# Rotary keys and queries by one projection and a lane shuffle in a four-layer cross-attention kernel

## The chip, the cores and the metric

The kernel runs on one core of a Trainium2 chip. The metric is the device time of one execution in microseconds, as the median of three runs. A core has TensorE (PE; PEld is its weight load), VectorE (DVE), ScalarE (ACT), GpSimd (POOL) and SyncE (SP, which here issues DMAs). Each takes its own list of instructions in order, and they wait for one another by semaphores.

## The reference

Four layers, each with cross-attention and a feed-forward part, on x of 16 batches x 112 tokens x 256, with a context of 16 x 375 x 256. All is float32. The attention of layer l is added to x with a gate:

```python
x = x + tanh(g_xattn[l]) * attention_l(layernorm(x), ctx)   # l = 0..3
x = x + tanh(g_ffn[l])   * ffn_l(layernorm(x))
# layer 0: 8 heads of 32; then layernorm(q + out) through a KAN layer:
#   silu(y) @ base_w.T + b_splines(y) @ scaled_spline_w.T   (8 bases per input)
# layer 1: 16 heads of 64, mask over keys
# layer 2: 16 heads of 16, rotary positions on q and k:
q = q * cos + rotate_half(q) * sin      # rotate_half(x) = [-x[8:], x[:8]] in each head
k = k * cos + rotate_half(k) * sin
# layer 3: 16 heads of 16, additive mask on the scores
```

The feed-forward parts (a tree of soft decisions, a dense mixture, two routed mixtures) are not touched.

## The kernel before

`attention_stage` builds one layer's attention for all engines; the Python loops are unrolled. `batches` goes over t = -1 .. 15 and one or two more. In iteration t the attention of batch t runs, the projections of batch t + 1 are made, and the output of batch t - 1 (in layer 0 also of t - 2) is finished.

Heads are worked in groups of four: four groups in layers 2 and 3, two in layer 0. In group i TensorE's `body` issues, in this order: `scores` of the next group (four products into the four banks of `sc_ps`), `pv` of the group before, and then three turns (`turn`, L723: four transposes of probabilities each) with the projections that `CYCLES` names between them. `CYCLES[layer][i][pos]` lists the uses that stand at place pos: before the first turn (0), after turn 0 (1), after turn 1 (2), after turn 2 (3). The names: `k`, `v`, `q` are projections; `kr` and `qr` are the same projections with the rows of the weights exchanged within each head, so that their result is the rotary partner; `xT` is the transpose of the normalized x; `rt` that of the reciprocal row sums; `out` the output projection; `lnt` the transpose of layer 0's normalized residual; `kan` its KAN product (a silu part, L679, and 16 spline parts, L683). `LAG` says to which batch each belongs.

All turns and uses take their PSUM room from `full_ps`, three banks handed out in turn over the list (`ring`). `bank_free` makes TensorE wait before each use until what was last in its bank has been copied out (`copied`).

Who copies: ACT copies k, v, q, xT and rt and turn 0 of each group; DVE copies turns 1 and 2 (`copy_turn`), and in layer 2 k, kr, q and qr, each in one instruction that adds the bias and multiplies by the cosine or sine table (L994, L1001). GpSimd adds the two products to kT (`rope_add`, L528), and DVE adds those of q and writes the two halves (`halve_q`). ACT's order in a group of layers 2 and 3 is: exponentials 0 and 1, copy of turn 0, exponentials 2 and 3, then the copies of places 1 to 3. DVE's is: row maxima (L1041; with a mask L1035), in group 0 `divide_o` and `norm_stats`, the use of place 1, turn 1, in group 0 `norm_apply` (L965), the use of place 2, turn 2, the use of place 3. GpSimd's in an iteration is: `power` (L516, the inverse root for the norm), rope_add of chunk 0, `add_bias` (L522), `spread` (the reciprocals, L535), rope_add of chunk 1. Without a mask the scores of a group wait until all four exponentials have read `sc_ps`; with one they wait for DVE's masked copy.

SyncE only loads the context, two batches ahead, and weights of later stages.

The lines of the profile are those of the code below.

Of the kernel before, what the change touches and what calls it, by code (L numbers as in the profile page):

```python
# [22 lines left out]
P = 128  # L23
# [156 lines left out]
def batches(eng, body, tail):  # L180

    for b in range(-1, B + tail):
# [7 lines left out]
        [[], [], [("lnt",), ("kan",)], [("v", 1, 0), ("qtok",), ("v", 2, 0), ("rest",)]]],  # L190
# [15 lines left out]
LAG = {"k": 1, "kr": 1, "v": 1, "xT": 1, "q": 1, "qr": 1, "qtok": 1, "rt": 0, "turn": 0, "out": -1,  # L206
# [10 lines left out]
def attention_stage(core, layer, heads, hd, scale, rope=False, mask=None, kan=False, moe=None):  # L217
# [21 lines left out]
    for i in range(NG):  # L239
# [9 lines left out]
    plain = lambda u: u[0] in ("k", "kr", "v", "xT", "qtok") or (u[0] == "q" and layer == 1)  # L249
    on_bank = {r: [j for j in jobs if plain(j) and bank_of[j] == r] for r in range(BANKS)}  # L250
    kv = [j for j in jobs if j[0] in ("k", "kr", "v")]
# [3 lines left out]
        (u[0] in ("k", "q") and not rope)  # L255
# [5 lines left out]
    with ExitStack() as ctx:  # L261
# [8 lines left out]
        if rope:  # L270
            wqr, wkr = room([P, DC, DQ]), room([P, DC, DQ])
            weights += [(wqr, "wqrT"), (wkr, "wkrT")]
# [4 lines left out]
        if rope:  # L277
            bqr, bkr = room([P, QC]), room([P, QC])
            cos, sin = room([P, SK]), room([P, SK])
            small += [(bqr, "bqr"), (bkr, "bkr"), (cos, "cos"), (sin, "sin")]  # L280
# [56 lines left out]
        if rope:  # L337
            rot_a, rot_b = sb("rot_a", [P, 2, SK]), sb("rot_b", [P, 2, SK])
            qrot_a, qrot_b = sb("qrot_a", [P, DC, S]), sb("qrot_b", [P, DC, S])
# [51 lines left out]
        if rope:  # L391
            s_ropek = sig("rope_k_ready", QC)
            s_rope_q = sig("rope_q_parts", 2 * DC)
            s_qsum = sig("q_summed", 1)
# [14 lines left out]

        def job(j, b):  # L410

            return s_job.sem, s_job.at(b, index_of[j])

        def copied(u, b):
# [5 lines left out]
            if kind == "q" and rope:  # L420
                return s_rope_q.sem, s_rope_q.at(b, DC - 1)
            if kind == "qr":
                return s_rope_q.sem, s_rope_q.at(b, 2 * DC - 1)
# [56 lines left out]
        with nc.Block() as block:  # L480
# [30 lines left out]
            def _(pool):  # L511
# [12 lines left out]
                def rope_add(b, par, c):  # L524

                    for kind in ("k", "kr"):
                        pool.wait_ge(*copied((kind, c), b))
                    pool.tensor_tensor(kT[:, par, c, :], rot_a[:, c, :], rot_b[:, c, :], ALU.add)\  # L528
                        .then_inc(s_ropek.sem, 1)

# [43 lines left out]
                def body(t, par):  # L574
# [18 lines left out]
            def _(pe):  # L593
# [13 lines left out]
                def run_use(u, t, par):  # L607
# [4 lines left out]
                    if kind in ("k", "kr"):  # L612
                        if u == kv[0]:
                            in_ctx(pe, b, par)
                        w = wk if kind == "k" else wkr
                        for c in range(DC):
                            mm = pe.matmul(use_ps[:, 0:SK], w[:, c, u[1] * P:(u[1] + 1) * P],  # L617
# [17 lines left out]
                    elif kind in ("q", "qr"):  # L635
                        if kind == "q":
                            pe.wait_ge(*copied(("xT",), b))
                        w = wq if kind == "q" else wqr
                        for i in range(qn):
                            f = u[1] + i  # L640
                            for c in range(DC):
                                mm = pe.matmul(use_ps[:, i * S:(i + 1) * S], w[:, c, f * P:(f + 1) * P],
# [28 lines left out]
                    else:  # L671
                        kan_output(b, use_ps[0:S, 0:D])

                def kan_output(b, kan_ps):
# [3 lines left out]
                    for c in range(DC):  # L678
                        pe.matmul(kan_ps, silu[:, c, :], base_w[:, c, :], start=(c == 0), stop=False)  # L679
                    for c in range(DC):  # L680
# [6 lines left out]
                def scores(b, par, i):  # L687
                    chunk = q_of(par, head(i, 0))[3]
                    if rope:
                        pe.wait_ge(s_ropek.sem, s_ropek.at(b, chunk))  # L690
# [55 lines left out]
                def body(t, par):  # L746
                    for i in range(NG):
# [1631 lines left out]
```

## Time and profile before

| | |
|---|---|
| median of 3 runs | 3092.79 us (3087.96 to 3093.75) |
| the profiled execution | 3098.28 us, span 3096.4 us |
| PE busy in the span | 2832.2 us (91%) |
| DVE, ACT, POOL busy | 1588.6 us, 1277.7 us, 520.8 us |
| attention of layer 0 | from about 14 to 435 us: PE 368.48 of 421 us |
| attention of layer 2 | from about 1444 to 1842 us: PE 382.03 of 398 us, POOL 56.01, clock 0.99 |
| attention of layer 3 | from about 2324 to 2690 us: PE 336.94 of 366 us, clock 0.96 |

The busy time of an engine is the sum of its instructions. The clock is TensorE's granted clock as a share of full speed. The last three lines come from the view that gives busy times in chosen stretches of the span.

### The profile page before, as it was taken

What the parts mean: (1) busy time and instruction counts of PE and PEld (TensorE: products, weight loads), DVE (VectorE), ACT (ScalarE), POOL (GpSimd) and SP (SyncE); (2) the same over time, 40 slices, a digit from 0 to 9 for tenths busy, and PEclk for the clock granted to TensorE, in tenths of its full rate; (3) what the DMA queues carried; (4) which work ended last, traced back from release to release, by engine and by line L of the source; (5) the groups of instructions that cost most, each with busy time, mean ns of one, the idle gap of its engine ahead of it and who ended that gap; (6) DMA issues with size and microseconds to landing.
All of it is one profiled execution on the core that took longest, in us unless ns stands there. A gap on an engine that the chain in (4) does not pass through costs nothing. (4 is left out here: it accounts for less than half of the span.)

```text
span 3096.4 us, 58811 instructions
## 1 busy us (share of the span) xinstructions
PE 2832.2 (91%) x20592; PEld 2152.5 (70%) x20592; DVE 1588.6 (51%) x4239; ACT 1277.7 (41%) x3555; POOL 520.8 (17%) x441
## 2 busy tenths in 40 slices
PE   6999968999999999698999975999988999859998
PEld 4777645666666666556766655999985667648887
DVE  4767634555555555345777763233326777532222
ACT  4676621444344334212555541333336666412221
POOL 1555530000000000000111110222210000002222
PEclk8999989999999999589999995999999999769999
DMA  3000010000000000010000003999971000048887
GB/s 111 16 16 21 6 66 2 12 12 7 12 12 12 7 12 1 28 38 7 16 16 20 18 7 106 348 328 327 329 246 33 22 22 17 23 142 279 280 285 222
DMA packets 92887, 269.66 MB, mean 87 GB/s; under 512 B 25977, under 2 KB 51722, under 8 KB 78314
## 3 DMA queue, kind: packets, MB, share of 16 engines
q1 hardware_dynamic: 75434, 244.63, 23.1%
q0 software_dynamic: 13632, 18.62, 3.0%
q10 hardware_dynamic: 3616, 3.67, 0.4%
q8 instruction: 130, 2.13, 0.3%
q14 instruction: 75, 0.61, 0.1%
HBM read 250.23 MB, written 18.48 MB: 87 GB/s over the span
## 5 line engine op out<-in xcount | busy, mean ns | idle before, releaser
L723 PEld LDWEIGHTS a_full_ps<-ident,a_probs 112*125 112x125 f32 x2688 | 369.7, 190 | 153.2 <-issue 59.6
L2146 PE MATMUL e_ab_ps<-e_xT,e_w 128*128 128x128 f32 (+1 forms) x3968 | 467.3, 278 | 5.4 <-DMA e_w<-in_L3f_w 2.3
L2146 PEld LDWEIGHTS e_ab_ps<-e_xT,e_w 128*128 128x128 f32 (+1 forms) x3968 | 453.6, 189 | 24.4 <-issue 11.9
L723 PE MATMUL a_full_ps<-ident,a_probs 112*125 112x112 f32 x2688 | 422.2, 282 | 30.1 <-ACT a_kT L788 9.5
L1061 DVE COPY a_pT<-a_full_ps 125x448 f32<-125x448 f32 x448 | 277.4, 621 | 281.0 <-PE a_full_ps L723 279.7
L821 ACT ACTIVATE a_probs<-a_masked,a_negmax 112x375 f32<-112x375 f32 x512 | 305.4, 598 | 278.0 <-DVE a_negmax L1035 278.0
L617 PE MATMUL a_full_ps<-attention_room 128*128 128x375 f32 x1024 | 371.0, 490 | 1.1 <-DVE a_v L1006 0.6
L625 PE MATMUL a_full_ps<-attention_room 128*125 128x256 f32 (+1 forms) x960 | 331.1, 474 | 8.5 <-ACT a_qT L813 3.1
L821 ACT ACTIVATE a_probs<-a_sc_ps,a_negmax 112x375 f32<-112x375 f32 x384 | 217.9, 579 | 125.7 <-DVE a_negmax L1041 125.6
L1035 DVE CUSTOM_DVE_ANT_0 a_masked<-a_sc_ps,a_mask_add 112x375 f32<-112x375 f32 x512 | 249.8, 544 | 36.8 <-PE a_sc_ps L710 36.4
L741 PEld LDWEIGHTS a_o_ps<-a_pT,a_v 125*32 125x32 f32 (+1 forms) x5376 | 164.7, 118 | 125.4 <-issue 124.3
L710 PE MATMUL a_sc_ps<-a_kT,a_qT 32*112 32x375 f32 (+1 forms) x1792 | 241.5, 513 | 3.3 <-ACT a_probs L821 3.2
L617 PEld LDWEIGHTS a_full_ps<-attention_room 128*128 128x128 f32 x1024 | 182.9, 194 | 80.7 <-issue 5.7
L2157 PE MATMUL e_y_ps<-e_w,e_hid 128*128 128x256 f32 x992 | 233.0, 383 | 0.0
L625 PEld LDWEIGHTS a_full_ps<-attention_room 128*125 128x125 f32 x960 | 167.2, 189 | 90.5 <-issue 66.2
L516 POOL TENSOR_TENSOR a_rstd<-a_rstd,minus_half 112x1 f32<-112x1 f32 x64 | 35.1, 549 | 1113.8 <-DVE a_rstd L958 1106.7
L741 PE MATMUL a_o_ps<-a_pT,a_v 125*32 125x112 f32 (+1 forms) x5376 | 216.6, 266 | 5.8 <-DVE a_pT L1061 3.8
L2190 ACT ACTIVATE e_silu<-e_ab_ps,e_b 128x128 f32<-128x128 f32 x280 | 102.4, 367 | 242.7 <-PE e_ab_ps L2146 227.8
L2157 PEld LDWEIGHTS e_y_ps<-e_w,e_hid 128*128 128x128 f32 x992 | 179.9, 190 | 32.2 <-issue 12.1
L1041 DVE TENSOR_REDUCE a_negmax<-a_sc_ps 112x2 f32<-112x750 f32 x192 | 171.3, 934 | 58.8 <-PE a_sc_ps L710 58.8
L2080 POOL DMA_INDIRECT p_sums<-e_y_out,p_put x71 | 112.6, 1586 | 512.1 <-DVE e_y_out L2230 288.7
L2217 DVE SCALAR_TENSOR_TENSOR e_hid<-e_ab_ps,e_b,e_silu 128x128 f32<-128x128 f32 x280 | 97.9, 351 | 172.1 <-ACT e_silu L2190 172.1
(247 smaller groups left out, 3654.2 us busy)
## 6 DMA issues: line engine op xcount, KB each, us to landing
e_w<-in_L2f_w SPq DMA_DIRECT2D x105, 1024.0 KB, 6.9
e_w<-in_L3f_w SPq DMA_DIRECT2D x72, 704.0 KB, 5.3
e_w<-in_L3f_w SPq DMA_DIRECT2D x36, 768.0 KB, 5.8
attention_room<-in_ctxT SPq DMA_DIRECT2D x64, 375.0 KB, 3.0
e_b<-in_L2f_b SPq DMA_DIRECT2D x35, 128.0 KB, 8.4
p_rows<-r_kept SPq DMA_DIRECT2D x32, 112.0 KB, 1.9
p_sums<-x_all ACTq DMA_DIRECT2D x2, 1792.0 KB, 18.1
attention_room<-in_L0x_spline_wT SPq DMA_DIRECT2D x1, 2048.0 KB, 9.9
```

Of the source, the lines that this page charges most:

```text
L617: mm = pe.matmul(use_ps[:, 0:SK], w[:, c, u[1] * P:(u[1] + 1) * P], ctxT[:, par, c, :], start=(c == 0), stop=(c == DC - 1))
L625: mm = pe.matmul(use_ps[0:KT, 0:v_width], ctxT[:, par, c, k * KT:(k + 1) * KT], wv[:, c, part * v_width:(part + 1) * v_width], start=(c == ...
L710: pe.matmul(sc_ps[:, a, 0:SK], lhs, kT[r:r + k, par, c, :], start=True, stop=True)\
L723: mm = pe.transpose(full_ps[0:KT, bank_of["turn", i, k], (j % 4) * S:(j % 4 + 1) * S], probs[:, i % 2, a, t * KT:(t + 1) * KT], ident[0:S, ...
L741: mm = pe.matmul(o_ps[a % WIDE * VW:(a % WIDE + 1) * VW, block * S:(block + 1) * S], v[:, par, t, head(i, a), :], pT[:, i % 2, KC * a + t, :],
L821: act.activation(probs[:, i % 2, a, 0:SK], src, ACT.Exp, bias=negmax[:, m:m + 1], scale=-1.0 if mask else 1.0, accum_out=rowsum[:, par, n: ...
L1035: dve.tensor_tensor_reduce(out=masked[:, i % 2, a, :], in0=sc_ps[:, a, 0:SK], in1=bias, scale=-1.0, scalar=FLT_MAX, op0=ALU.add, op1=ALU.m ...
L1041: dve.tensor_reduce(negmax[:, m:m + 2], sc_ps[:, 2 * a:2 * a + 2, 0:SK], AX.X, ALU.max, negate=True).then_inc(s_max.sem, 1)
L1061: dve.tensor_copy(pT[:, i % 2, 4 * k:4 * (k + 1), :], full_ps[0:KT, bank_of["turn", i, k], 0:4 * S] .rearrange("p (j s) -> p j s", j=4)).t ...
L2080: pool.indirect_dma_start(plan.sums, bass.IndirectOffsetOnAxis(plan.put[:, t:t + 1], 0), y_out[:, t % 2, :], None, compute_op=ALU.add).the ...
L2146: mm = pe.matmul(ab_ps[0:rows[f], (par * FC + f) % RING, i * SLOTS:(i + 1) * SLOTS], w[:, par, c, f * P:f * P + rows[f]], xT[:, c, :], sta ...
L2157: mm = pe.matmul(y_ps[:, par, 0:D], hid[0:rows[f], f, :], w2[0:rows[f], par, f, :], start=(f == 0), stop=(f == FC - 1))
```

## The change

In layer 2, `kr` and `qr` and their weights go away. ACT copies k and q with their bias from PSUM to SBUF (`k_raw`, `q_raw`). DVE makes the partners from these copies by `stream_shuffle`, which exchanges partitions within each 32 (`PARTNERS`; `partners_k`, `partners_q`), after turn 1 of the group in which k or q stands. GpSimd multiplies by the cosines and by the sines and adds, for k (`rope_add`) and now for q too (`rope_q`, between add_bias and spread). The list of layer 2 becomes nearly that of layer 3.

In layers 2 and 3 (`divided`), ACT copies the use of place 1 between exponentials 1 and 2 instead of after exponential 3. In layer 0, the silu part of `kan` stands ahead of `lnt`, and the spline parts follow lnt; with that kan and lnt exchange their banks.

```diff
-        [[], [], [("lnt",), ("kan",)], [("v", 1, 0), ("qtok",), ("v", 2, 0), ("rest",)]]],
+        [[], [], [("kan",), ("lnt",)], [("v", 1, 0), ("qtok",), ("v", 2, 0), ("rest",)]]],
...
-    2: [[[], [("k", 0)], [("kr", 0)], [("xT",)]],
-        [[], [("q", 0)], [("out",)], [("qr", 0)]],
-        [[], [("v", 0, 0)], [("v", 1, 0)], [("v", 2, 0)]],
-        [[], [("k", 1)], [("kr", 1)], [("rt",)]]],
+    2: [[[], [("k", 0)], [("v", 0, 0)], [("xT",)]],
+        [[], [("q", 0)], [("out",)], []],
+        [[], [("v", 1, 0)], [], []],
+        [[], [("k", 1)], [("v", 2, 0)], [("rt",)]]],
...
+PARTNERS = [p // 16 * 16 + (p + 8) % 16 for p in range(32)]
...
                 def rope_add(b, par, c):
-                    for kind in ("k", "kr"):
-                        pool.wait_ge(*copied((kind, c), b))
+                    step = lambda k: (s_ropek.sem, s_ropek.at(b, c * ROPE_STEPS + k))
+                    pool.wait_ge(*copied(("k", c), b))
+                    pool.sem_inc(s_tick[3].sem, 1)
+                    pool.tensor_tensor(rot_a[:, c, :], k_raw[:, c, :], cos[:], ALU.mult).then_inc(s_ropek.sem, 1)
+                    pool.wait_ge(s_kpart.sem, s_kpart.at(b, c))
+                    pool.sem_inc(s_tick[3].sem, 1)
+                    pool.tensor_tensor(rot_b[:, c, :], k_partner[:, c, :], sin[:], ALU.mult).then_inc(s_ropek.sem, 1)
+                    pool.wait_ge(*step(ROPE_SIN))
+                    pool.sem_inc(s_tick[3].sem, 1)
                     pool.tensor_tensor(kT[:, par, c, :], rot_a[:, c, :], rot_b[:, c, :], ALU.add)\
                         .then_inc(s_ropek.sem, 1)
+                def rope_q(b):
+                    table = lambda t: t[:, 0:S].unsqueeze(1).to_broadcast([P, DC, S])
+                    pool.wait_ge(s_qf.sem, s_qf.at(b, QC - 1))
...
+                    pool.tensor_tensor(qrot_a[:], q_raw[:], table(cos), ALU.mult).then_inc(s_ropeq.sem, 1)
+                    pool.wait_ge(s_qpart.sem, s_qpart.at(b))
...
+                    pool.tensor_tensor(qrot_b[:], q_partner[:], table(sin), ALU.mult).then_inc(s_ropeq.sem, 1)
...
+                    pool.tensor_tensor(qfull[:], qrot_a[:], qrot_b[:], ALU.add).then_inc(s_ropeq.sem, 1)
...
                         add_bias(t + 1)
+                    if rope and exists(t + 1):
+                        rope_q(t + 1)
...
                     else:
-                        kan_output(b, use_ps[0:S, 0:D])
+                        kan_silu(b, use_ps[0:S, 0:D])
...
                             for u in uses_at(t, i, pos):
                                 run_use(u, t, par)
+                            if ("kan",) in cycles[i][pos] and exists(t - 2):
+                                kan_splines(t - 2)
...
                     if kind == "k":
                         f = u[1]
-                        act.activation(kT[:, par, f, :], use_ps[:, 0:SK], ACT.Identity,
+                        if rope and has(b, 1):
+                            act.wait_ge(*rotated(b - 1, f))
+                            act.sem_inc(s_tick[0].sem, 1)
+                        act.activation(k_raw[:, f, :] if rope else kT[:, par, f, :], use_ps[:, 0:SK], ACT.Identity,
...
+                        if divided:
+                            copies(t, par, i, 1)
                         for group in groups:
                             exps(*group, (2, 3))
...
-                        for pos in range(1, TURNS + 1):
+                        for pos in range(2 if divided else 1, TURNS + 1):
                             copies(t, par, i, pos)
...
+                def partners_k(b, c):
+                    if has(b, 1):
+                        dve.wait_ge(*rotated(b - 1, c))
+                        dve.sem_inc(s_tick[1].sem, 1)
+                    dve.wait_ge(*copied(("k", c), b))
+                    dve.sem_inc(s_tick[1].sem, 1)
+                    dve.stream_shuffle(k_partner[:, c, :], k_raw[:, c, :], PARTNERS).then_inc(s_kpart.sem, 1)
...
                 def halve_q(b, par):
                     if rope:
-                        dve.wait_ge(s_rope_q.sem, s_rope_q.at(b, 2 * DC - 1))
...
-                        dve.tensor_tensor(qfull[:], qrot_a[:], qrot_b[:], ALU.add).then_inc(s_qsum.sem, 1)
-                        dve.wait_ge(s_qsum.sem, s_qsum.at(b))
+                        dve.wait_ge(s_ropeq.sem, s_ropeq.at(b, ROPE_SUM))
...
                         if exists(t):
                             copy_turn(t, i, 1)
+                        if rope and exists(t + 1):
+                            if ("k", 0) in cycles[i][1]:
+                                partners_k(t + 1, 0)
+                            if ("k", 1) in cycles[i][1]:
+                                partners_k(t + 1, 1)
+                            if ("q", 0) in cycles[i][1]:
+                                partners_q(t + 1)
                         if i == 0 and exists(t + 1):
                             norm_apply(t + 1)
```

`rotated(b, c)` is the semaphore value at which GpSimd's sum for chunk c of k is done. `partners_q` is made like `partners_k`, in one shuffle of 224 columns.

## Rows read from the trace of the kernel before

**Rows 1.** Timeline, layer 2, one batch: start us, us, engine, line, operation, [idle before].
```profile
1604.94 0.90 PE L710 MATMUL a_sc_ps<-a_kT,a_qT 32*112 32x375 f32 x8
...
1607.01 1.44 PE L617 MATMUL a_full_ps<-attention_room 128*128 128x375 f32 x4
...
1608.29 0.59 PE L723 MATMUL a_full_ps<-ident,a_probs 112*125 112x112 f32 x4
1608.71 1.44 PE L617 MATMUL a_full_ps<-attention_room 128*128 128x375 f32 x4
...
1610.41 0.35 PE L632 MATMUL a_full_ps<-ident,a_xn 112*128 112x112 f32 x2
...
1610.70 0.90 PE L710 MATMUL a_sc_ps<-a_kT,a_qT 32*112 32x375 f32 x8
...
1616.70 0.90 PE L710 MATMUL a_sc_ps<-a_kT,a_qT 32*112 32x375 f32 x8
...
1623.28 0.90 PE L710 MATMUL a_sc_ps<-a_kT,a_qT 32*112 32x375 f32 x8
...
1629.04 0.90 PE L710 MATMUL a_sc_ps<-a_kT,a_qT 32*112 32x375 f32 x8
```

**Rows 2.** Timeline, layer 2, last batch, without projections.
```profile
1821.84 0.90 PE L710 MATMUL a_sc_ps<-a_kT,a_qT 32*112 32x375 f32 x8
...
1825.31 0.58 ACT L821 ACTIVATE a_probs<-a_sc_ps,a_negmax 112x375 f32<-112x375 f32 x1
...
1826.68 0.90 PE L710 MATMUL a_sc_ps<-a_kT,a_qT 32*112 32x375 f32 x8 [1.74 <-ACT a_probs L821]
```

**Rows 3.** Timeline, layer 2, group 0 of the batch of rows 1, DVE and GpSimd.
```profile
1608.91 0.55 POOL L516 TENSOR_TENSOR a_rstd<-a_rstd,minus_half 112x1 f32<-112x1 f32 x1 [2.73 <-DVE a_rstd L958]
...
1609.28 0.61 DVE L1061 COPY a_pT<-a_full_ps 125x448 f32<-125x448 f32 x1
1609.81 0.41 DVE L965 TENSOR_SCALAR a_xn<-x_all,a_mv,a_rstd 112x256 f32<-112x256 f32 x1
...
1610.95 0.98 POOL L528 TENSOR_TENSOR a_kT<-a_rot_a,a_rot_b 128x375 f32<-128x375 f32 x1 [1.49 <-DVE a_rot_b L994]
```

**Rows 4.** Timelines of DVE and GpSimd, layer 0, at two places.
```profile
70.50 1.11 DVE L1134 SCALAR_TENSOR_TENSOR a_near<-a_sq,a_near 128x896 f32<-128x896 f32 x1
...
70.62 2.53 POOL L544 TENSOR_TENSOR a_sq<-a_near 128x896 f32<-128x896 f32 x1
...
207.75 1.67 POOL L544 TENSOR_TENSOR a_sq<-a_near 128x896 f32<-128x896 f32 x1
...
208.26 1.31 DVE L965 TENSOR_SCALAR a_xn<-x_all,a_mv,a_rstd 112x256 f32<-112x256 f32 x1
```

**Rows 5.** Timeline, layer 3, end of one group 0.
```profile
2492.36 1.04 PE L625 MATMUL a_full_ps<-attention_room 128*125 128x256 f32 x4
...
2493.05 0.56 ACT L788 ACTIVATE a_kT<-a_full_ps,attention_room 128x375 f32<-128x375 f32 x1
2493.44 0.41 DVE L965 TENSOR_SCALAR a_xn<-x_all,a_mv,a_rstd 112x256 f32<-112x256 f32 x1
...
2493.76 0.66 PE L723 MATMUL a_full_ps<-ident,a_probs 112*125 112x112 f32 x4 [0.35 <-ACT a_kT L788]
...
2494.25 0.35 PE L632 MATMUL a_full_ps<-ident,a_xn 112*128 112x112 f32 x2
```

**Rows 6.** Timeline, layer 0, lnt and the uses around it.
```profile
221.87 0.38 PE L669 MATMUL a_full_ps<-ident,a_resn 112*128 112x112 f32 x2 [0.78 <-DVE a_resn L1103]
...
222.09 1.03 PE L679 MATMUL a_full_ps<-attention_room,a_silu 128*112 128x256 f32 x4
...
222.96 7.10 PE L683 MATMUL a_full_ps<-attention_room,a_bases 128*112 128x256 f32 x32
...
230.10 0.48 DVE L1077 SCALAR_TENSOR_TENSOR x_all<-a_full_ps,gates,x_all 112x256 f32<-112x256 f32 x1 [4.06 <-PE a_full_ps L683]
...
230.32 1.04 PE L625 MATMUL a_full_ps<-attention_room 128*125 128x256 f32 x4
...
231.19 1.03 PE L647 MATMUL a_full_ps<-attention_room,a_xT 128*112 128x256 f32 x4
```

More of the change, by code:

```diff
@@ L204 @@
 BANKS, TURNS = 3, 3
-LAG = {"k": 1, "kr": 1, "v": 1, "xT": 1, "q": 1, "qr": 1, "qtok": 1, "rt": 0, "turn": 0, "out": -1,
+ROPE_COS, ROPE_SIN, ROPE_SUM, ROPE_STEPS = 0, 1, 2, 3
+PARTNERS = [p // 16 * 16 + (p + 8) % 16 for p in range(32)]
+LAG = {"k": 1, "v": 1, "xT": 1, "q": 1, "qtok": 1, "rt": 0, "turn": 0, "out": -1,
        "oback": -1, "lnt": -1, "kan": -2}
@@ L248, in attention_stage @@
     index_of = {j: i for i, j in enumerate(jobs)}
-    plain = lambda u: u[0] in ("k", "kr", "v", "xT", "qtok") or (u[0] == "q" and layer == 1)
+    plain = lambda u: u[0] in ("k", "v", "xT", "qtok") or (u[0] == "q" and layer == 1)
     on_bank = {r: [j for j in jobs if plain(j) and bank_of[j] == r] for r in range(BANKS)}
-    kv = [j for j in jobs if j[0] in ("k", "kr", "v")]
+    kv = [j for j in jobs if j[0] in ("k", "v")]
     v_width = min(DQ, 512)
@@ L254, in attention_stage @@
     on_scalar = lambda u: u[0] in ("xT", "rt") or (u[0] == "v" and layer != 1) or \
-        (u[0] in ("k", "q") and not rope)
+        u[0] in ("k", "q")
     OC = heads * hd // P
@@ L277, in attention_stage @@
         if rope:
-            bqr, bkr = room([P, QC]), room([P, QC])
             cos, sin = room([P, SK]), room([P, SK])
-            small += [(bqr, "bqr"), (bkr, "bkr"), (cos, "cos"), (sin, "sin")]
+            small += [(cos, "cos"), (sin, "sin")]
         if hd == 16:
@@ L634, in run_use @@
                         mm.then_inc(s_job.sem, 1)
[L635 to L638, printed above, removed]
+                    elif kind == "q":
+                        pe.wait_ge(*copied(("xT",), b))
                         for i in range(qn):
@@ L679, in kan_output, with kan_splines @@
                         pe.matmul(kan_ps, silu[:, c, :], base_w[:, c, :], start=(c == 0), stop=False)
+                def kan_splines(b):
+                    kan_ps = full_ps[0:S, bank_of[("kan",)], 0:D]
                     for c in range(DC):
@@ L689, in scores @@
                     if rope:
-                        pe.wait_ge(s_ropek.sem, s_ropek.at(b, chunk))
+                        pe.wait_ge(*rotated(b, chunk))
                     elif layer != 1:
@@ L796, in copy_use @@
                         if has(b, 1):
-                            act.wait_ge(*job([j for j in jobs if j[0] in ("q", "qr", "qtok")][-1], b - 1))
+                            act.wait_ge(*job([j for j in jobs if j[0] in ("q", "qtok")][-1], b - 1))
                         act.activation(xT[:, :, :], use_ps[:, 0:DC * S].rearrange("p (c s) -> p c s", c=DC),
@@ L988, in copy_use @@
                     dve.wait_ge(*job(u, b))
-                    if kind in ("k", "kr"):
-                        f = u[1]
-                        if has(b, 1):
-                            dve.wait_ge(s_ropek.sem, s_ropek.at(b - 1, f))
-                        dst, bias, table = (rot_a, bk, cos) if kind == "k" else (rot_b, bkr, sin)
-                        dve.scalar_tensor_tensor(out=dst[:, f, :], in0=use_ps[:, 0:SK], scalar=bias[:, f:f + 1],
-                                                 in1=table[:], op0=ALU.add, op1=ALU.mult).then_inc(free, 1)
-                    elif kind in ("q", "qr"):
-                        if has(b, 1):
-                            dve.wait_ge(s_qsum.sem, s_qsum.at(b - 1))
-                        dst, bias, table = (qrot_a, bq, cos) if kind == "q" else (qrot_b, bqr, sin)
-                        for c in range(DC):
-                            dve.scalar_tensor_tensor(out=dst[:, c, :], in0=use_ps[:, c * S:(c + 1) * S],
-                                                     scalar=bias[:, c:c + 1], in1=table[:, 0:S], op0=ALU.add,
-                                                     op1=ALU.mult).then_inc(s_rope_q.sem, 1)
-                    elif kind == "v":
+                    if kind == "v":
                         _, k, part = u
```

55 lines of the change are left out of this document (31 added, 24 removed).

## The prediction

> **What bounds the kernel now.** I read the busy table of the page first: TensorE is busy for nine tenths of the span, so the question is always which wait of TensorE goes. Then I read the timeline of one batch in each of the three attention layers that the change touches, because a share over the span says nothing about one loop. Times below are counted from the start of the scores (L710) that open a group; each group ends where the next scores start.
>
> Layer 2 [rows 1]: a batch is four groups of 5.76, 6.00, 6.58 and 5.76 us, 24.10 us in all (1604.94 to 1629.04), and TensorE runs its list nearly without a gap. From scores to the first projection 2.07 us, k 1.28, a turn 0.42, then kr and another turn, the transpose of xn (xT) 0.29. In the middle of the layer ACT and DVE have slack.
>
> A second limit is visible only where the projections run out [rows 2]: there scores follow scores after 4.84 us, with TensorE waiting 1.74 us for the exponentials. sc_ps is one buffer: scores, row maxima, exponentials 0 and 1, the copy of a turn, exponentials 2 and 3 (the third starts at 3.47), next scores. Nothing shortens this loop, and whatever ACT does inside it lengthens it.
>
> Layer 3 [rows 5] has the same list without kr and qr. In groups 0 and 3 turn 2 needs the bank that k used, and ACT copies k only after exponential 3. The v product starts at 2492.36 and, being 0.87 long [rows 6], ends at 2493.23; the turn starts at 2493.76. That is 0.53 us lost; group 3, with rt in place of xT, has the same, and I take 0.5 there.
>
> Layer 0 [rows 6]: the transpose lnt waits for the residual (0.78 us of it as a gap before L669) while the silu product, whose input is there, stands behind it.
>
> **Layer 2, part by part.** Removed from TensorE per batch: two kr products of 1.28 us and qr (taken as 1.0), about 3.5 us. Removed from DVE: four multiply-adds of 375 columns, four of 112 and the q sum. Added on ACT: k copied twice, 0.56 us each [rows 5], and q in two pieces, which I take as 0.6 together. On DVE: three shuffles. On GpSimd: two more operations of 375 columns for each k chunk (0.98 each [rows 3]) and three of 224 for q, about 0.6 each by columns. GpSimd then works some 9 us of a batch, and its k and q are due 2 to 10 us after they are ready. They are hidden, unless they hinder DVE. The new waits of ACT and DVE for the sums of the batch before are met a batch's length earlier.
>
> The shuffle is in no row. Below, I bound it by a 256-column DVE instruction, 0.41, above by the 448-column copy, 0.61 [rows 3]; for 375 columns I take 0.5. The Trainium skill (VectorE: DVE Perf Modes, "The perf-mode tier table") gives a shuffle about 2400 ns for 2048 elements; an estimate from it is 0.44 us for 375, and the sum would be 1 us shorter by it.
>
> Now the groups, with the new list of projections:
>
> Group 3 (k, v, rt). TensorE needs 5.76 less kr 1.28 plus v 0.87, or 5.35. The exponential loop takes k's copy in: k ends at 3.51, its copy at about 4.12, exponential 2 moves from 3.47 to about 4.05, and 4.84 becomes about 5.4. I take 5.4.
>
> Group 1 (q, out). TensorE would need 6.00 less 1.0, but the loop has 4.84 plus two q copies less a small overlap, about 5.35. The loop decides.
>
> Group 2 (v). The loop with one v copy of 0.37 is 5.2, and TensorE needs less than 4.4. The loop decides.
>
> Group 0 (k, v, xT) is where a new wait comes. xT needs norm_apply on DVE. Before, norm_apply runs from 4.87 to 5.28 and TensorE wants it at 5.47 [rows 1, 3], so nobody waits. Now TensorE wants xT at 5.06, and the shuffle of k stands in front of norm_apply: copy_turn starts at about 4.0, ends and lets the shuffle in at 4.55, norm_apply could start at 5.05. But GpSimd has ended its power at 4.52 [rows 3] and is multiplying k by the cosines until about 5.5, and the two engines exclude each other for such operations: in layer 0 the same L965 that takes 0.41 us alone takes 1.31 beside L544 and ends 0.15 after it [rows 3, 4]. So norm_apply ends at 5.65 to 6.0, I take 5.7; xT follows 0.15 later and the scores 0.29 after that: 6.15. Does the sine multiplication slip in first? Rows 4 have such a meeting: L1134 on DVE asks at 70.50 while L549 ends, ends itself at 71.61, and the L544 that GpSimd had queued takes 2.53 us instead of 1.67. DVE got in between, so I let DVE in after the cosines. Its delay of group 0 also delays copy_turn(0,2), which group 1 needs only 0.83 after its start, so nothing more.
>
> Sum: 6.15 + 5.35 + 5.2 + 5.4 = 22.1 against 24.1, 2.0 us a batch, and 15 full batches: 30 us. The bounds for group 0 are 5.75 (no meeting, shuffle 0.41) and 7.1 (DVE also waits for the sines), which gives 36 and 16 us. The start of the stage I take as even: two half-clock products less, against ACT and three GpSimd operations in place of one ahead of the first scores. The end, where no batch follows, does not change. The halving of q waits on GpSimd now; q is copied at 4.1 of group 1, three times 0.6 later it is summed, and the halving comes at about 2.7 of group 2. What stands behind that wait (two copies of turns and so the next pv) is safe by about 2 us.
>
> **Layer 3.** k's copy moves ahead of exponentials 2 and 3. TensorE's turn 2 then follows v at once: 0.5 us saved in group 3. In group 0 the next limit is xT again: norm_apply ends at 2493.85, xT starts at 2494.25 and could start at about 2494.0, so I count 0.25, not 0.53 [rows 5]. The later exponentials do no harm, because scores here wait for DVE's masked copies and turn 1 of the next group comes several us later. 0.75 a batch, 15 batches: 11 us. Bounds: 0.3 (a second wait behind the bank) and 1.0, so 4 to 15.
>
> **Layer 0.** The silu product (222.09 to 222.96, 0.87) moves into the wait: lnt stays where it is, the splines start 0.87 earlier. The banks of kan and lnt are exchanged by this. v(1) now needs the bank of kan, which is free when DVE has updated x_all, at 230.10 + 0.48 = 230.58, and TensorE wants it at 230.32 [rows 6]; 0.26, and 0.1 more for wait and weight load that were hidden, come back. Before, that update had the whole v product (0.87, to 231.19) as cover. Net 0.5 us in 13 batches and 0.87 in the last two: 8 us. Bounds 0 and 12.
>
> **Total.** The profiled execution took 3098.28 us (span 3096.4), 5.5 above the median of 3092.79. Its stages lose 30 + 11 + 8 = 49 us: 3049 for such an execution, and taken off the median 3044.
>
> **Rivals.**
> 1. GpSimd keeps the port through cosines and sines (its instructions follow each other within 0.05 us). Group 0 becomes 7.1 and layer 2 saves 16 us: 3092.8 - 16 - 19 = 3058. Against it stands the meeting at 70.5.
> 2. The shuffles are held off by GpSimd too. Then the shuffle of group 0 ends at about 5.9, norm_apply at 6.2, the group at 6.65; group 3 gets 0.15 longer. Layer 2 saves 1.35 a batch, 20 us: 3054. No row shows a DVE instruction of that kind beside GpSimd. The Trainium skill (SBUF, State Buffer, "Who interferes with whom") says that a DVE instruction with one SBUF input outside the two-port modes does not contend, and its tier table gives the shuffle only the 1x mode; by it this rival falls and the sum stays at 22.1.
> 3. Everything is cover: norm_apply gets through ahead of the cosines, layer 3 gets its full 1.0, layer 0 its 0.87. 36 + 15 + 12 = 63: 3030, the lower side.
> 4. The orders give less than they say: the waits of layers 0 and 3 are replaced by others of the same length (0 and 4 us left). 30 + 4: 3059.
> 5. Slower: the shuffle is dear. Be D its time for 375 columns. Above 0.6 it adds D - 0.75 in group 0, above 1.0 D - 1.0 in group 3 (copy_turn(3,2) then misses the next pv), and in group 1 about 0.6 D - 0.8: 2.55 less than 2.6 D in all. The forecast gain of 3.3 a batch is gone at D = 2.25; slower by over 0.2% needs 2.4, or 6.4 ns a column, where DVE's rows have 1.4 to 1.6 with the fixed part. At D = 3 the time would be 3044 + 15 x 5.25 = 3123.
>
> **Chances.** Forecast 0.45, rivals 0.14, 0.11, 0.12, 0.12 and 0.05 in order; 0.01 for the unforeseen. The range runs from 3028 to 3064: it holds the forecast with its bounds and rivals 1 to 4 mostly. A measurement of this kernel tells about 0.2% (6 us) from no change. Faster 0.92, same 0.03, slower 0.05.
>
> **What will show it.** Distances between the scores in layer 2: about 6.15, 5.35, 5.2, 5.4. In groups 1 and 2 the scores should be released by the exponentials (a gap before L710 put down to ACT), which the steady part has nowhere now. Before xT a wait for DVE's xn, and L965 at 0.6 us or more in layer 2. In layer 3 the wait for ACT's k gone, and the batch 0.75 us shorter. In layer 0 the batch 0.5 us shorter, and v(1) waiting for x_all. I am wrong if group 0 stays below 5.8 or above 6.6, if groups 1 and 2 fall below 5, or if any layer's batch is longer than before.

## The result and the profile after

| | before | after |
|---|---|---|
| median | 3090.86 us (3087.96 to 3093.75, 4 runs) | 3044.99 us (3041.45 to 3048.90, 4 runs) |
| profiled execution (span) | 3098.28 us (3096.4) | 3048.90 us (3047.1) |
| PE, DVE busy | 2832.2, 1588.6 us | 2778.5, 1549.9 us |
| ACT, POOL busy | 1277.7, 520.8 us | 1301.9, 608.1 us |

The ratio is 0.9852, with a 95% interval of 0.9835 to 0.9869: 46 us faster. The forecast was 3044, taken as 49 us off the median of 3092.79; the fourth run of the kernel before has moved that median to 3090.86.

I read the after trace as I read the other: by the distance from one scores to the next. Steady values in us, good to 0.01 or 0.02, with the span from the stage's first scores to its last:

| | before | forecast | after | span before, after |
|---|---|---|---|---|
| layer 2, groups 0 to 3 | 5.76, 6.00, 6.58, 5.76 | 6.15, 5.35, 5.2, 5.4 | 5.92, 5.33, 5.09, 5.48 | 375.17, 342.70 |
| layer 2, a batch | 24.10 | 22.1 | 21.82 | |
| layer 3, groups 0 to 3 | 5.95, 4.94, 4.11, 5.95 | 5.7, 4.94, 4.11, 5.45 | 5.72, 4.94, 4.11, 5.40 | 325.62, 314.13 |
| layer 0, a batch | 22.79 | 22.3 | 22.33 | 348.94, 336.55 |

One batch of layer 2 in the timeline, the counterpart of [rows 1] and [rows 3]: start us, us, engine, line, operation, [idle before]. Scores are now L735, turns L748, xT L656, norm_apply L1001.

```profile
1606.55 0.85 POOL L530 TENSOR_TENSOR a_rot_a<-a_k_raw,attention_room 128x375 f32<-128x375 f32 x1
1606.61 0.59 DVE L1038 STREAM_SHUFFLE a_k_partner<-a_k_raw 128x375 f32<-128x375 f32 x1
1607.09 0.46 DVE L1001 TENSOR_SCALAR a_xn<-x_all,a_mv,a_rstd 112x256 f32<-112x256 f32 x1
1607.38 0.88 POOL L533 TENSOR_TENSOR a_rot_b<-a_k_partner,attention_room 128x375 f32<-128x375 f32 x1
1607.70 0.39 PE L656 MATMUL a_full_ps<-ident,a_xn 112*128 112x112 f32 x2 [0.37 <-DVE a_xn L1001]
1608.01 0.90 PE L735 MATMUL a_sc_ps<-a_kT,a_qT 32*112 32x375 f32 x8
...
1612.50 0.60 ACT L855 ACTIVATE a_probs<-a_sc_ps,a_negmax 112x375 f32<-112x375 f32 x1
...
1613.34 0.90 PE L735 MATMUL a_sc_ps<-a_kT,a_qT 32*112 32x375 f32 x8
...
1618.42 0.90 PE L735 MATMUL a_sc_ps<-a_kT,a_qT 32*112 32x375 f32 x8 [0.72 <-ACT a_probs L855]
...
1622.54 0.57 ACT L855 ACTIVATE a_probs<-a_sc_ps,a_negmax 112x375 f32<-112x375 f32 x1
...
1623.09 0.58 ACT L855 ACTIVATE a_probs<-a_sc_ps,a_negmax 112x375 f32<-112x375 f32 x1
...
1623.90 0.90 PE L735 MATMUL a_sc_ps<-a_kT,a_qT 32*112 32x375 f32 x8
```

Group 0 started at 1602.09, so norm_apply is asked for at 5.00, ends at 5.46 and xT starts at 5.61, after a wait of 0.37 that before did not have. In groups 1, 2 and 3 the scores follow the end of the fourth exponential by 0.23 or 0.24 (1612.50 + 0.60 against 1613.34; 1623.09 + 0.58 against 1623.90), as where the projections run out in [rows 2]. The exponential loop has become the bound. Only group 2 shows it as a gap of TensorE. In group 3 the margin is small: TensorE's own list would let the scores start about 0.1 us earlier (turn 2 starts at 1623.07; with 0.42 for it and 0.29 for rt the scores could follow at 1623.78). In group 3 k's copy (0.57, at 1622.07) moved the third exponential to 4.12 after the scores; without a copy it is at 3.47.

The view of waits, TensorE, 1500 to 1750 us (waited for: us in total, times, longest), has these two on top:

```profile
PE a_sc_ps L735 <- ACT a_probs L855: 8.7, 12, 0.7
PE a_full_ps L656 <- DVE a_xn L1001: 4.0, 11, 0.4
```

Both waits were forecast. One sign did not come: norm_apply should have taken 0.6 us or more in layer 2, and takes 0.46.

Groups of instructions of the same stretch (xcount | busy us, mean ns | idle before) give the prices that no row of before had:

```profile
L536 POOL TENSOR_TENSOR a_kT<-a_rot_a,a_rot_b 128x375 f32<-128x375 f32 x23 | 22.6, 981 | 4.1 <-POOL a_rot_b L533 4.1
L530 POOL TENSOR_TENSOR a_rot_a<-a_k_raw,attention_room 128x375 f32<-128x375 f32 x22 | 20.3, 924 | 10.6 <-ACT a_k_raw L818 10.6
L1038 DVE STREAM_SHUFFLE a_k_partner<-a_k_raw 128x375 f32<-128x375 f32 x22 | 12.9, 586 | 0.0
L1047 DVE STREAM_SHUFFLE a_q_partner<-a_q_raw 128x224 f32<-128x224 f32 x12 | 4.9, 412 | 0.5 <-issue 0.4
```

Layer 3, end of one group 0, the counterpart of [rows 5]. The turn (2490.01) follows v (2489.13 + 0.88) at once, and what is late next is xT, by 0.17:

```profile
2489.13 1.04 PE L649 MATMUL a_full_ps<-attention_room 128*125 128x256 f32 x4
...
2490.01 0.59 PE L748 MATMUL a_full_ps<-ident,a_probs 112*125 112x112 f32 x4
2490.21 0.41 DVE L1001 TENSOR_SCALAR a_xn<-x_all,a_mv,a_rstd 112x256 f32<-112x256 f32 x1
...
2490.77 0.38 PE L656 MATMUL a_full_ps<-ident,a_xn 112*128 112x112 f32 x2 [0.17 <-DVE a_xn L1001]
```

Layer 0, the counterpart of [rows 6]. The silu product fills the wait, and v(1) now waits for the update of x_all:

```profile
214.22 1.03 PE L701 MATMUL a_full_ps<-attention_room,a_silu 128*112 128x256 f32 x4
215.16 0.38 PE L691 MATMUL a_full_ps<-ident,a_resn 112*128 112x112 f32 x2
215.37 7.10 PE L708 MATMUL a_full_ps<-attention_room,a_bases 128*112 128x256 f32 x32
...
223.05 1.13 PE L649 MATMUL a_full_ps<-attention_room 128*125 128x256 f32 x4 [0.15 <-DVE x_all L1113]
```

**Something is given back.** The spans add up to 32.5 + 11.5 + 12.4 = 56 us, the two executions differ by 49. The start of layer 0 varies from one execution to the next: its first scores came 2.45 later in this one (23.32 against 20.87; over all kernels they lie between 20.6 and 23.4), and the kernel with ACT's new order alone, whose layer 0 is that of the kernel before, has a span of 345.77 there, not 348.94. From the ninth scores to the last the layer takes 265.39 us before and 259.85 after, and each other kernel with the same order in layer 0 is within 0.06 of one or the other; so some 5.5 of the 12.4 us are the steady gain, and a part of the rest is such variation. What is really given back stands at the end of layer 2: from its last scores to the first product of the routing after it, 20.99 us (1831.76 to 1852.75) became 25.77 (1786.42 to 1812.19):

```profile
1786.42 0.90 PE L735 MATMUL a_sc_ps<-a_kT,a_qT 32*112 32x375 f32 x8
...
1788.01 1.13 PE L748 MATMUL a_full_ps<-ident,a_probs 112*125 112x112 f32 x8
1790.15 0.66 PE L748 MATMUL a_full_ps<-ident,a_probs 112*125 112x112 f32 x4 [1.01 <-ACT a_pT L861]
1791.62 1.35 PE L766 MATMUL a_o_ps<-a_pT,a_v 125*32 125x112 f32 x24 [0.81 <-DVE a_pT L1097]
1792.89 2.86 PE L748 MATMUL a_full_ps<-ident,a_probs 112*125 112x112 f32 x12
```

With the new list, turn 2 of group 2 has the bank of turn 0 and waits for ACT's copy of it (1.01; in the steady part 0.17). Before, the twelve transposes ran together. Then TensorE goes at half clock: pv, the product of probabilities and v, takes 1.35 instead of 0.78. The view of stretches (length, PE busy, ..., then the granted clock) has 0.50 for 1792 to 1800, the 1.2 GHz level, after a stretch in which TensorE was busy for 4.18 of 6 us:

```profile
1786.00:1792.00 6.00, 4.18 (x59) 3.04 (x60) 4.24 (x7) 2.76 (x9) 0.20 (x1) 0.93 0.00 0
1792.00:1800.00 8.00, 7.11 (x65) 5.49 (x55) 1.98 (x4) 0.90 (x2) 0.20 (x1) 0.50 0.01 2
```

The kernel with `rest` first (below), whose last scores start at 1786.57, runs the same work after them and stays at full clock. But it had been at the lower level just before, which the changed kernel had not (1.00 for 1776 to 1786):

```profile
1776.00:1786.00 10.00, 8.10 (x88) 5.54 (x88) 6.16 (x10) 5.72 (x19) 1.58 (x2) 0.83 0.01 2
1786.00:1792.00 6.00, 4.18 (x60) 3.01 (x63) 4.24 (x7) 2.91 (x11) 0.05 (x1) 1.00 0.00 0
```

Over all profiled executions: the eight with the new list all have the wait of 1.01 there; behind it six go at half clock to the end of the layer, one (copies last) for a part of it, and two (`rest` first, all together) stay at full clock. The three with the old list do not wait there, and both later pv take 0.78.

### The profile page after: what moved, and what is told of

Same layout as the page of the kernel before. It is cut to its first block and busy times, and to the rows that moved or that the text cites. A ratio compares the mean times of both kernels' runs of the same rounds, so it can differ in the third digit from the quotient of the medians.

```text
span 3047.1 us, 58569 instructions
## 1 busy us (share of the span) xinstructions
PE 2778.5 (91%) x20336; PEld 2123.1 (70%) x20336; DVE 1549.9 (51%) x4191; ACT 1301.9 (43%) x3619; POOL 608.1 (20%) x553
## 5 line engine op out<-in xcount | busy, mean ns | idle before, releaser
L748 PEld LDWEIGHTS a_full_ps<-ident,a_probs 112*125 112x125 f32 x2688 | 372.4, 190 | 123.6 <-issue 64.3
L748 PE MATMUL a_full_ps<-ident,a_probs 112*125 112x112 f32 x2688 | 420.0, 281 | 19.4 <-ACT a_pT L861 8.4
L641 PE MATMUL a_full_ps<-attention_room 128*128 128x375 f32 x896 | 324.8, 491 | 0.7 <-DVE a_v L1027 0.6
L735 PE MATMUL a_sc_ps<-a_kT,a_qT 32*112 32x375 f32 (+1 forms) x1792 | 241.2, 512 | 20.9 <-ACT a_probs L855 13.7
L641 PEld LDWEIGHTS a_full_ps<-attention_room 128*128 128x128 f32 x896 | 160.6, 195 | 70.9 <-issue 4.5
```

Source lines behind the costliest of these rows:

```text
L641: mm = pe.matmul(use_ps[:, 0:SK], wk[:, c, u[1] * P:(u[1] + 1) * P], ctxT[:, par, c, :], start=(c == 0), stop=(c == DC - 1))
L735: pe.matmul(sc_ps[:, a, 0:SK], lhs, kT[r:r + k, par, c, :], start=True, stop=True)\
L748: mm = pe.transpose(full_ps[0:KT, bank_of["turn", i, k], (j % 4) * S:(j % 4 + 1) * S], probs[:, i % 2, a, t * KT:(t + 1) * KT], ident[0:S, ...
```

## The experiments

Ratios are against the kernel before, run beside them: its median was 3091.96 for the two parts alone and for the norm and the cosines moved singly, 3091.11 for both moved, the two shuffles, v(1) and `rest`, 3090.86 for the new list with the copies last and for all of it together. A median or an interval tells 46 us easily, but not 2 or 3; where runs of a kernel overlap those of the changed kernel (3041.45 to 3048.90), I say so, and the distances between scores decide. My theory: TensorE's list was the bound in layer 2, the exponential loop over sc_ps (4.84 us plus ACT's copies) bounds groups 1 to 3 after the change, norm_apply bounds group 0, and the three parts of the change add up. The rivals of the forecast stand in the expectations.

**One part at a time: layer 0's order.** The kernel before with the exchange of kan and lnt and the split of `kan_output`, as in the diff of the change.

> The kernel before with layer 0's change alone (silu product ahead of lnt, splines after it). My theory: the silu product fills the wait for the residual, and v(1) then waits for the update of x_all; the period of layer 0 goes from 22.80 to 22.34 us as in the changed kernel, and the time falls by 7 to 8 us (0.25%). Rival (the gain of the changed kernel in layer 0 comes with its other edits): 22.80 stays, no difference.

Measured: 3084.48 us against 3091.96, ratio 0.9973 [0.9963, 0.9983]. Layer 0's batch is 22.34 (before 22.79), layers 2 and 3 are as before. Layer 0 is worth 7.5 us by itself, and the rival fell.

**One part at a time: ACT's order.** The kernel before with

```diff
+                        if divided:
+                            copies(t, par, i, 1)
                         for group in groups:
                             exps(*group, (2, 3))
-                        for pos in range(1, TURNS + 1):
+                        for pos in range(2 if divided else 1, TURNS + 1):
```

> The kernel before with ACT's new order alone in layers 2 and 3 (the use of place 1 copied between exponentials 1 and 2). My theory: layer 3's batch goes from 20.95 to 20.2 us, as in the changed kernel (11 us); in layer 2, still with kr and qr, only group 2 gains, because its third turn waits for ACT's copy of v(0): 6.58 to about 6.2, so 24.1 to 23.7 (6 us). Together about 17 us. Rival (the order matters in layer 2 only with the new list, and in layer 3 the wait moves elsewhere): under 5 us.

Measured: 3075.35, ratio 0.9952 [0.9936, 0.9969], 16.6 us for the expected 17. Layer 3's batch 20.18 (span 314.46): its whole gain. Layer 2's groups 5.76, 6.01, 6.00, 5.76: group 2 loses 0.58, since v(0) is copied early (1610.32) and turn 2, which before waited 0.34 for the two v copies, no longer waits. Its rows:

```profile
1610.32 0.39 ACT L794 ACTIVATE a_v<-a_full_ps 125x256 f32<-125x256 f32 x1
...
1611.46 0.59 PE L723 MATMUL a_full_ps<-ident,a_probs 112*125 112x112 f32 x4
```

**The new list without ACT's new order.** The changed kernel with these lines taken out again:

```diff
-                        if divided:
-                            copies(t, par, i, 1)
...
-                        for pos in range(2 if divided else 1, TURNS + 1):
+                        for pos in range(1, TURNS + 1):
```

> The changed kernel without ACT's new order: in layers 2 and 3 the use of place 1 is copied after exponential 3 again. My theory: layer 3 returns to 20.95 (11.5 us). In layer 2 the new list needs the early copy more than the old one: k is copied at 4.6 of group 0 instead of 3.6, the shuffle and norm_apply follow it, groups become about 6.5, 5.7, 4.84 and 5.95, 23.0 in place of 21.82 (18 us). Together about 29 us above the changed kernel, 3074. Rival (the two edits add up): layer 2 loses no more than the 0.58 a batch that the order gained in the old kernel: 9 us, and 20 us together.

Measured: 3083.77, ratio 0.9970 [0.9958, 0.9982], 38.8 us above the changed kernel. Layer 3 is back at 20.94. Layer 2's groups are 6.80, 5.91, 4.84, 6.05, 23.60 in all: the new list by itself takes only 0.5 us off a batch, the order by itself (above) 0.57, both together 2.28. The rows of group 0 (from 1618.32) show why:

```profile
1622.88 0.59 ACT L818 ACTIVATE a_k_raw<-a_full_ps,attention_room 128x375 f32<-128x375 f32 x1
1623.62 0.66 PE L748 MATMUL a_full_ps<-ident,a_probs 112*125 112x112 f32 x4 [0.49 <-ACT a_k_raw L818]
1623.65 0.59 DVE L1036 STREAM_SHUFFLE a_k_partner<-a_k_raw 128x375 f32<-128x375 f32 x1
1624.13 0.52 DVE L999 TENSOR_SCALAR a_xn<-x_all,a_mv,a_rstd 112x256 f32<-112x256 f32 x1
1624.80 0.38 PE L656 MATMUL a_full_ps<-ident,a_xn 112*128 112x112 f32 x2 [0.52 <-DVE a_xn L999]
```

k is copied after four exponentials, turn 2 waits for its bank, the shuffle waits for the copy, and norm_apply stands behind the shuffle. The two parts are one edit in layer 2. The rival (at most 20 us) fell, and my 29 us missed too: group sizes too short by 0.6 a batch, 38.8 us measured. In time the list alone is worth nothing that can be told: this kernel also holds layer 0's new order, and gains 7.1 us where that order alone gains 7.5. Layer 2's span is 4.9 us shorter (370.28 for 375.17), and 3.0 us are lost at its end (24.01 for 20.99). So the three parts of the change do not add up as I said: about 7.5 for layer 0, 16.6 for ACT's order, 0 for the list, and some 22 of the 46 us only for list and order together.

**Group 0: who makes norm_apply late?** Two things could: DVE's shuffle ahead of it, and GpSimd's cosines beside it. I took away the one, the other, and both. First norm_apply ahead of the shuffle:

```diff
+                        if i == 0 and exists(t + 1):
+                            norm_apply(t + 1)
...
                         if rope and exists(t + 1):
                             if ("k", 0) in cycles[i][1]:
                                 partners_k(t + 1, 0)
...
-                        if i == 0 and exists(t + 1):
-                            norm_apply(t + 1)
```

> The changed kernel with norm_apply ahead of the shuffle of k(0) on DVE in layer 2. Group 0 is 5.92 us in the changed kernel. Theory A (the place of the shuffle is what makes xT late): norm_apply starts 0.5 us earlier, group 0 becomes about 5.45, 7 us less in all. Theory B (port: GpSimd's multiplication by cosines starts 0.05 us before norm_apply can, and holds it off until it ends): norm_apply asks at 4.57, ends again 0.15 after the cosines, at 5.46; group 0 stays at 5.92 and the time at that of the changed kernel. I expect B for this edit alone, since both causes hold and either one suffices.

Then `rope_add` of chunk 0 behind `add_bias` on GpSimd:

```diff
-                    if rope and exists(t + 1):
-                        rope_add(t + 1, 1 - par, 0)
...
                         add_bias(t + 1)
                     if rope and exists(t + 1):
+                        rope_add(t + 1, 1 - par, 0)
```

> The changed kernel with GpSimd's three operations for k(0) behind add_bias, so that GpSimd is idle when norm_apply runs. If the port alone makes xT late (theory B alone): group 0 falls from 5.92 to about 5.45, 7 us. If the shuffle alone does (theory A), or both do: norm_apply takes 0.41 instead of 0.46 us and group 0 falls by 0.05 at most, under 1 us in all. I expect the latter.

And both:

> The changed kernel with both: norm_apply ahead of the shuffle, and GpSimd's work on k(0) behind add_bias. My theory (two causes side by side, each enough): group 0, which stayed at 5.92 with the first and fell to 5.85 with the second, now falls to where the exponential loop with k's copy holds it, 5.48 as in group 3. 0.44 a batch, 15 batches: 6.5 us below the changed kernel, about 3038. Rival (a third cause, such as power's result or the wait before the transpose): stays above 5.75.

| | norm_apply started, ended | xT started | group 0 | batch | time | ratio |
|---|---|---|---|---|---|---|
| changed kernel | 5.00, 5.46 | 5.61 | 5.92 | 21.82 | 3044.99 | 0.9852 |
| norm first | 4.53, 5.46 | 5.60 | 5.91 | 21.83 | 3044.35 | 0.9852 [0.9835, 0.9869] |
| cosines later | 5.00, 5.39 | 5.53 | 5.85 | 21.75 | 3042.66 | 0.9841 [0.9825, 0.9857] |
| both | 4.53, 4.94 | 5.09 | 5.48 | 21.34 | 3037.30 | 0.9823 [0.9807, 0.984] |

Starts and ends count from the start of the scores of group 0; norm_apply starts, in the record, when it has its input and its turn, and lasts longer than 0.41 where it is held. "Norm first" and "cosines later" share one comparison (before 3091.96), "both" has another (before 3091.11). With the norm first, DVE is held by the cosines, and ends 0.15 after them:

```profile
1607.24 0.85 POOL L530 TENSOR_TENSOR a_rot_a<-a_k_raw,attention_room 128x375 f32<-128x375 f32 x1
1607.31 0.93 DVE L1001 TENSOR_SCALAR a_xn<-x_all,a_mv,a_rstd 112x256 f32<-112x256 f32 x1
```

With both, nothing stands before it:

```profile
1607.21 0.41 DVE L1001 TENSOR_SCALAR a_xn<-x_all,a_mv,a_rstd 112x256 f32<-112x256 f32 x1
...
1607.35 0.57 ACT L855 ACTIVATE a_probs<-a_sc_ps,a_negmax 112x375 f32<-112x375 f32 x1
1607.54 0.57 DVE L1038 STREAM_SHUFFLE a_k_partner<-a_k_raw 128x375 f32<-128x375 f32 x1
1607.77 0.38 PE L656 MATMUL a_full_ps<-ident,a_xn 112*128 112x112 f32 x2
...
1608.16 0.90 PE L735 MATMUL a_sc_ps<-a_kT,a_qT 32*112 32x375 f32 x8
```

Either cause alone holds the group at 5.85 or 5.91; only without both does it fall, to 5.48. The times agree: "norm first" lies among the runs of the changed kernel, "cosines later" (3040.56 to 3045.00) overlaps them, "both" (3035.41 to 3040.94) lies below all of them. There the exponential loop takes over: 1607.35 + 0.57 + 0.24 is 1608.16. An experiment that removes one of two causes, each enough by itself, shows nothing of the other.

**What a shuffle costs there.** An extra shuffle ahead of the real one, into a spare tile:

```diff
+                    dve.stream_shuffle(k_spare[:, c, :], k_raw[:, c, :], PARTNERS)
                     dve.stream_shuffle(k_partner[:, c, :], k_raw[:, c, :], PARTNERS).then_inc(s_kpart.sem, 1)
```

> The changed kernel with every shuffle of k done twice (the first into a spare tile). This prices the shuffle where it stands, for the slower rival of the prediction. By its formula one more shuffle (0.48 us from start to start) adds about its length to group 0, since it passes the cosines: 5.92 to 6.37; group 3 is untouched up to 1.0 us of shuffles, or grows by 0.05. 7 us more in all. Rival (the shuffle is hidden behind the cosines): group 0 grows by less than 0.1. Second rival (it holds up pv in group 3): group 3 grows by 0.4 too, 14 us.

Measured: 3051.50, ratio 0.9867 [0.985, 0.9883], 6.5 us above the changed kernel for the expected 7; its four runs spread from 3047 to 3058. Group 0 is 6.33, up by 0.41; groups 1 to 3 stay. The two start 0.49 apart, the first wholly beside the cosines and no longer for it; the norm, started 0.47 after the second and past the cosines, takes 0.40:

```profile
1614.12 0.85 POOL L531 TENSOR_TENSOR a_rot_a<-a_k_raw,attention_room 128x375 f32<-128x375 f32 x1
1614.18 0.58 DVE L1039 STREAM_SHUFFLE a_k_spare<-a_k_raw 128x375 f32<-128x375 f32 x1
...
1614.67 0.58 DVE L1040 STREAM_SHUFFLE a_k_partner<-a_k_raw 128x375 f32<-128x375 f32 x1
...
1615.14 0.40 DVE L1002 TENSOR_SCALAR a_xn<-x_all,a_mv,a_rstd 112x256 f32<-112x256 f32 x1
```

The extra shuffle adds 0.49, and 0.07 of it is the hold by the cosines that the norm no longer meets.

**Is group 2 bound by the exponential loop?** v(1) copied after the exponentials again, in layer 2 only:

```diff
-                        if divided:
+                        early = divided and not (rope and cycles[i][1][0][0] == "v")
+                        if early:
                             copies(t, par, i, 1)
```

> The changed kernel with ACT's copy of v(1), the use of place 1 in group 2 of layer 2, back behind exponential 3. My theory (the loop over sc_ps bounds groups 1 and 2, TensorE's list does not): group 2 falls from 5.09 to 4.84, the length that the loop has without any copy; 3.7 us less. Rival (TensorE's list or the bank of the third turn bounds group 2): 5.09 stays.

Measured: 3041.67, ratio 0.9842 [0.9825, 0.9858], with runs that overlap those of the changed kernel. Group 2 is 4.81, the others stay. TensorE still waits for the exponentials:

```profile
1616.63 0.59 ACT L855 ACTIVATE a_probs<-a_sc_ps,a_negmax 112x375 f32<-112x375 f32 x1
...
1617.46 0.90 PE L735 MATMUL a_sc_ps<-a_kT,a_qT 32*112 32x375 f32 x8 [0.45 <-ACT a_probs L855]
```

So the loop bounds the group, and its bare length is the 4.84 of [rows 2]. For group 1, with the two q copies in the loop, no run takes the copies out; there it rests on the rows. The early copy, needed for k, costs here 0.28.

**Layer 0's residue.** `rest` in front of v(1), so that the update has a turn as cover:

```diff
-        [[], [], [("kan",), ("lnt",)], [("v", 1, 0), ("qtok",), ("v", 2, 0), ("rest",)]]],
+        [[], [], [("kan",), ("lnt",)], [("rest",), ("v", 1, 0), ("qtok",), ("v", 2, 0)]]],
```

> The changed kernel with layer 0's empty place put ahead of v(1) instead of behind v(2), so that v(1) takes the bank of lnt, qtok that of turn 2 and v(2) that of kan. My theory (v(1) waits for the update of x_all): the wait goes, the second group of layer 0 falls from 14.13 to about 13.75, the period from 22.33 to about 21.95, 5 us less in all. Rival (qtok now waits for DVE's copy of turn 2 by as much): 22.33 stays or grows.

Measured: 3042.23, ratio 0.9843 [0.9827, 0.986]. The batch is 22.03, 0.30 less, a little short of expected; the time is 2.8 us less where I expected 5, with runs that overlap those of the changed kernel. The wait of v(1) is gone:

```profile
201.22 0.49 DVE L1113 SCALAR_TENSOR_TENSOR x_all<-a_full_ps,gates,x_all 112x256 f32<-112x256 f32 x1 [3.19 <-PE a_full_ps L708]
201.44 1.04 PE L649 MATMUL a_full_ps<-attention_room 128*125 128x256 f32 x4
```

**All of it together**: norm first, cosines later, v(1) after the exponentials, `rest` first.

> All improvements that the experiments point to on top of the changed kernel: norm_apply ahead of the shuffle, GpSimd's k(0) behind add_bias, v(1) of layer 2 copied after the exponentials, the empty place of layer 0 first. By my theory they touch different groups and add up: layer 2 at 5.48 + 5.33 + 4.84 + 5.48 = 21.13 (10 us), layer 0 at 21.95 (5 us): 3030, 0.980 of the kernel before. Rival (what is freed in one group is waited for in the next): 3038 or more.

Measured: 3024.98 us (3022.9 to 3034.2, 5 runs), ratio 0.9796 [0.9779, 0.9813] to the kernel before, 20 us below the changed kernel. Layer 2's groups are 5.48, 5.31, 4.81, 5.48 (21.08, span 331.47), layer 0's batch 22.02. By batches that is 15 x 0.74 + 13 x 0.3 = 15; its profiled execution also passed the end of layer 2 at full clock, in 22.50 us (1771.68 to 1794.18) in place of 25.77. The five runs fall into two groups: three took 3022.9 to 3025.0 at a mean granted clock of 0.942 or 0.943, two took 3033.5 and 3034.2 at 0.937. The median stands in the first, so the 20 us hold more than the batches give.

## Why the prediction was right

**Which wait goes, which comes (right).** TensorE's list was the bound in layer 2, the loop over sc_ps is it now in groups 1 to 3 (tested in group 2, where v copied late gives 4.81; read from the rows in groups 1 and 3), and norm_apply in group 0. Sizes: group 1 5.33 for 5.35, group 2 5.09 for 5.2, group 3 5.48 for 5.4. In group 2 the v copy displaces the third exponential by 0.26 start to start, not by its own 0.37; in group 3 the third exponential starts at 4.12, not 4.05.

**Group 0 (right mechanism, term too large).** Forecast 6.15, measured 5.92. norm_apply was asked for at 5.00 (said 5.05), the cosines held it and it ended 0.15 after them (1606.55 + 0.85 = 1607.40, and 1607.55), as the meeting in [rows 4] had it. The mis-sized term is the cosines: 0.98 from GpSimd's sum, measured 0.85 here (1.00 in group 3; mean 0.924). That is 0.13 of the 0.23; another 0.06 is their start (4.46 for 4.52), and 0.05 that I took 5.7 where the working gave 5.65. The hold by the cosines was thereby given 0.24 (5.7 against 5.05 + 0.41), and is worth 0.07: without it the group is 5.85. The shuffle alone already makes the group late, and so do the cosines alone (5.91); the prediction did not see that taking away one would bring next to nothing.

**Rival 1 (fell).** GpSimd had the sines queued behind the cosines (its record of them starts at 1607.38), yet norm_apply ended at 1607.55: DVE got in between. The sines took 0.88 for the usual 0.85 or so.

**Rival 2 (fell).** The shuffle takes 0.58 and 0.59 with the cosines beside it (1614.18, 1606.61) and 0.57 with GpSimd idle (in the kernel with the cosines later). The Trainium skill (SBUF, State Buffer, "Who interferes with whom") says that a DVE instruction with one SBUF input outside the two-port modes does not contend with GpSimd. The trace agrees, to within those 0.02 us.

**The shuffle's price.** Taken 0.5, measured 0.586 of duration and 0.48 from its start to the next instruction's, which is what stands in the sum. The estimate of 0.44 from the Trainium skill's figure (VectorE: DVE Perf Modes, "The perf-mode tier table") is below both. Two widths, 0.586 for 375 columns and 0.412 for 224, make 1.15 ns a column and 0.15 us fixed. Rival 5 needed 2.25 us and fell.

**Rival 3 (fell).** Group 0 was held until both causes were away (5.48), layer 3 gave 0.77 a batch and not 1.0, and in layer 0 v(1) waited until `rest` stood first.

**Rival 4 (fell).** ACT's order alone gave 16.6 us (by the spans of its one profiled execution 11.2 in layer 3 and 7.8 in layer 2) and layer 0's order 7.5, where the rival left 4 and 0.

**Layer 3 (right).** 0.25 in group 0 and 0.5 in group 3 were said; 0.23 and 0.55 came, 11.5 us for 11.

**Layer 0 (right).** 0.5 in a batch said, 0.45 came; 8 us said, 7.5 measured alone.

**Layer 2's sum (too small by a tenth).** 2.28 a batch for 2.0, 32.5 us of span for 30. The start of the stage, taken as even, is not: the first distance is 4.84 for 4.41, and the first batch gains only 0.7.

**The end of layer 2 (wrong).** "The end, where no batch follows, does not change" failed. In the two profiled executions with the new list that stayed at full clock there it is 1.5 us longer (20.99 to 22.50): 1.14 by the bank wait (the second pv starts 5.20 after the last scores, for 4.06), and 0.37 because GpSimd starts the first inverse root of the routing 1.48 after its input is there, for 1.11, for which no run gives a reason. The half clock adds up to 3.3 more. In the profiled execution that is 4.8 us, against 2.5 by which layer 2's sum was too small. What the two profiled executions gained, part by part: 9.9 us up to layer 0's last scores (12.4 of span less the later start), 2.9 from there to layer 2's first, 32.5 in layer 2, -4.8 at its end, -2.3 from there to layer 3's first scores, 11.5 in layer 3, -0.4 in the rest: 49.3, which is the difference of the spans. The 2.9 and -2.3 lie within what these parts vary over all profiled kernels (5 and 3.5 us). The forecast had 49, and so close a hit is luck: layer 2, layer 0 and layer 3 gave 4.9 more than was said for them, and the end of layer 2 took 4.8.

**What stays open.** Why the clock fell at that end in the changed kernel and, for the same list, not in the kernel with `rest` first. The wait precedes it in each, and no kernel without the wait loses the clock in that place; that the wait brings it about is argued, not shown, and two kernels with it keep the clock. A list with another bank for that turn was not tried. That layers 0, 2 and 3 do not act on each other is shown only within the 3.5 to 5 us by which the parts between them vary from one profile to the next.

## What to carry to other kernels

Write down, for each group, both the list of the bound engine and the loop over the buffer it waits for; when one shrinks the other decides, and the gain ends there. Two edits that sit on one chain (a product removed, its copy moved earlier) can be worth far more together than apart, 2.28 us a batch against 0.50 and 0.57 here, and two delays that overlap each hide the other's removal, so take away both. Follow a new list through the drain of the loop as well, since there the bank order shows waits that the steady part covers.

## What the runs showed of the hardware

- Half the granted clock (0.50, 1.2 GHz) at the end of layer 2, in which pv takes 1.35 us instead of 0.78, after a stretch with TensorE busy for 4.18 of 6 us; with the same 4.18 of 6 in the kernel with `rest` first, the clock stayed at 1.00, and that kernel had been at 0.83 in the 10 us before (the changed kernel at 1.00).
- A GpSimd multiplication of 128 x 375 is 0.85 us in group 0 and 1.00 in group 3 of the same batch, the sum of two such tiles 0.98.
- ACT and DVE instructions overlap their neighbours: durations of 0.57 to 0.59 (k's copy, the shuffle) put the next one off by 0.46 to 0.49, v's copy of 0.39 by 0.26 to 0.28. In a chain it is the distance of starts that adds.
